# The experts' gathered rows are turned on VectorE in 32x32 blocks instead of on TensorE, and the last product is written as three matmuls

## The chip, the core and the metric

The kernel runs on one core of a Trainium2 chip. Its engines are TensorE (PE, matmuls; PEld is its weight load), VectorE (DVE), ScalarE (ACT), GpSimd (POOL) and SyncE (SP, which only issues transfers). The metric is device time in microseconds. The kernel before takes 1703.79 us, the median of three runs (1703.66 to 1705.21).

## The reference

Input is x, 8 batches of 1024 rows of 256 values. Everything is fp32.

```
xn = layernorm(x)
out = x + attention(xn) + ffn(xn)

attention: layer norm with weights, 16 heads of 16, rope, softmax over 1024 keys, output projection
ffn:  affinity = softmax(xn @ gate_w)                    # 8 experts
      gating, index = top_k(affinity per expert, 256)    # each expert takes 256 rows of each batch
      x_sel = xn[index]
      h = silu(x_sel @ Wg[e]) * (x_sel @ Wu[e])          # 256 -> 512
      contrib = (h @ Wd[e]) * gating                     # 512 -> 256
      out[index] += contrib
```

## The kernel before, in words

The program is one instruction stream for each engine, written out by hand; engines wait for each other through counting semaphores. It has two parts. The first (to about 1126 us) is attention with the router. The second is the experts, and only this one changes.

The experts' work is cut into 32 units: 8 experts of 4 units, each unit 512 gathered rows (ST = 4 tiles of 128). `bp` is the unit's number in its expert. POOL gathers a unit's rows from the normalised rows in DRAM by four indirect transfers (L694) into one of two buffers `xs`, two units ahead, and scatters a unit's results with four accumulating indirect transfers (L705).

fp32 products are made of three products of fp32r parts: each operand is a high part (a cast) and a low part (the difference), and high x high, low x high and high x low are added. So each weight and each activation is split: ACT casts to the high part, DVE subtracts to get the low part.

For one unit the engines do this:
- PE, `turn(unit + 1)` (L1098): the next unit's rows must lie with their 256 values along the partitions. Eight 128x128 transposes write them into the two banks `xt_ps` (L1105).
- ACT and DVE, `turned` (L773, L1452): high and low part of the turned rows, `x_hi` and `x_lo`, two 128x512 operations each.
- PE, `gate_up(unit)` (L1108): for each of four chunks f of the 512 hidden values, 6 matmuls into a gate bank and 6 into an up bank, 512 columns each (L1118). The banks alternate with f, so chunk f waits for h of chunk f - 2 (`need(pe, h_done, FC * unit + f - 1)`).
- ACT takes silu of the gate (L786); DVE multiplies by up, h(f) (L1467); ACT casts, high(f) (L780); DVE subtracts, low(f) (L1459).
- PE, `down(unit)` (L1122): for each row tile t and chunk f, one matmul of 512 columns of the high part of h against both parts of the down weights side by side (L1129), and one of 256 columns of the low part (L1131). A row tile's bank has so two halves of 256 that must be added.
- ACT scales one half by the gating value (L795); DVE scales the other and adds, `y` (L1481). Then POOL scatters.
- In the first three units of each expert but the last, ACT casts one of the next expert's three weights at the end of the unit (`high_weights`, L771), and DVE subtracts (`low_weights`, L1450).

DVE's queue is in order, so where an operation stands in `expert_unit` (L1461) decides what it delays. PE's order in a unit is gate_up, turn of the next unit, down. In units 0 and 1 DVE also prepares the last batch's output projection (`invert`, `quarter_split`), which PE runs in four jobs of 12 matmuls (L946), two behind unit 0 and two behind unit 1, in the banks `xt_ps`.

Of the kernel before, what the change touches and what calls it, by code (L numbers as in the profile page):

```python
# [8 lines left out]
ALU = mybir.AluOpType  # L9
# [6 lines left out]
P = 128  # L16
# [6 lines left out]
NPART = 2  # L23
LANE = 64
LANES = P // LANE
NPAIR = HPG // LANES
# [90 lines left out]
def program(nc, ctx, g):  # L117
# [93 lines left out]
    def tall(half):  # L211
# [13 lines left out]
             [wide(k_stack[0][:, 1, :]), wide(k_stack[0][:, 0, :]), tall(q_stack[1][:, 1, :])]]  # L225
    wd_both = [parts_of[:, :, :].rearrange("p k (f n) -> p k f n", f=FC) for parts_of in (zn_lo, q_stack[1])]
    xs = [qk[:, 2 * i:2 * i + 2, :].rearrange("p i (t n) -> p (i t) n", n=D) for i in range(2)]
    x_hi, x_lo = (k_stack[1][:, i, :].rearrange("p (c n) -> p c n", c=DC) for i in range(2))
    silu, h = [probs[1][:, i, :] for i in range(2)], [probs[1][:, 2 + i, :] for i in range(2)]
    h_hi = parts[1][:, :, :, :].rearrange("p k a n -> p (k a) n")  # L230
# [6 lines left out]
    def rows_ps(t):  # L237

        return (d_ps[0], d_ps[1], g_ps[(FC - 1) % 2], u_ps[(FC - 1) % 2])[t]

# [5 lines left out]
    scattered = [sem(f"scattered{i}") for i in range(UNITS)]  # L246
    xt_full, x_high, x_split = sem("xt_full"), sem("x_high"), sem("x_split")
    gate_full, up_full, silu_done, h_done, h_high, h_split = (
        sem(n) for n in ("gate_full", "up_full", "silu_done", "h_done", "h_high", "h_split"))
    down_full, y_scaled, y_begun = sem("down_full"), sem("y_scaled"), sem("y_begun")  # L250

# [126 lines left out]
    LOW_CYCLE = (28, 29, 30)  # L378
    END_BANKS = {("wo", q): (q // 2, q % 2) for q in range(QUARTERS)}
    ROUTER_CYCLE = (9, 19)  # L380
# [260 lines left out]
    def _(pool):  # L641
# [122 lines left out]
    def _(act):  # L764
# [8 lines left out]
        def turned(unit):  # L773
            for c in range(DC):
                act.wait_ge(xt_full, DC * unit + c + 1)
                act.copy(x_hi[:, c, :], xt_ps[c]).then_inc(x_high, 1)

# [4 lines left out]
        def expert_unit(unit):  # L782
            e, bp = unit // UNITS, unit % UNITS
            for f in range(FC):
                act.wait_ge(gate_full, FC * unit + f + 1)
                act.activation(silu[f % 2], g_ps[f % 2], ACT.Silu).then_inc(silu_done, 1)  # L786
                if f > 0:
                    high(unit, f - 1)
            high(unit, FC - 1)
            if unit + 1 < E * UNITS:  # L790
                turned(unit + 1)
            need(act, scattered[(bp - 2) % UNITS], ST * DMA * (e + (bp >= 2)))
            for t in range(ST):
                act.wait_ge(down_full, ST * unit + t + 1)
                act.activation(y[unit % 2][t], rows_ps(t)[:, D:2 * D], ACT.Copy,  # L795
                               scale=gates_flat[:, e * COLS + bp * ST + t:e * COLS + bp * ST + t + 1]).then_inc(y_begun, 1)
            if bp < WEIGHTS and e + 1 < E:
                high_weights(e + 1, bp)
# [83 lines left out]
    def _(pe):  # L882
# [214 lines left out]

        def turn(unit):  # L1098
            pe.wait_ge(gathered[unit % 2], ST * DMA * (unit // 2 + 1))
            for c in range(DC):  # L1100
                need(pe, x_split, DC * unit + c - 1)
                if unit in (2, 3):
                    pe.wait_ge(side_free, end_jobs.done(("wo", 2 * (unit - 2) + c)))
                for t in range(ST):
                    last = pe.transpose(xt_ps[c][:, t * P:(t + 1) * P], xs[unit % 2][:, t, c * P:(c + 1) * P], ident_sb[:, :])  # L1105
                last.then_inc(xt_full, 1)

        def gate_up(unit):  # L1108
            k = unit // UNITS % 2
            pe.wait_ge(x_split, DC * unit + DC)  # L1110
            for f in range(FC):
                need(pe, h_done, FC * unit + f - 1)
                if f == (FC - 1) % 2:
                    need(pe, y_scaled, ST * unit)
                for w, bank, full in ((GATE, g_ps, gate_full), (UP, u_ps, up_full)):
                    for i, (wt, xt) in enumerate(((we_hi, x_hi), (we_lo, x_hi), (we_hi, x_lo))):
                        for c in range(DC):
                            last = pe.matmul(bank[f % 2], wt[k][w][:, c, f * P:(f + 1) * P], xt[:, c, :],  # L1118
                                             start=i == 0 and c == 0, stop=i == 2 and c == DC - 1)
                    last.then_inc(full, 1)  # L1120

        def down(unit):  # L1122
# [12 lines left out]

            for t in range(2):
                need(pe, y_scaled, ST * (unit - 1) + t + 1)
                part(t, range(FC - 2))
# [8 lines left out]
        turn(0)  # L1147
        weigh(NB - 1, STEPS - 2)
        weigh(NB - 1, STEPS - 1)
        for unit in range(E * UNITS):  # L1150
            if unit % UNITS == 0:
                pe.wait_ge(w_split, WEIGHTS * (unit // UNITS + 1))
            gate_up(unit)
            if unit + 1 < E * UNITS:
                turn(unit + 1)
            if unit == 0:
                pe.wait_ge(o_copied, NB * 2 * NG)
                pe.wait_ge(side_free, end_jobs.base)
            down(unit)
            for job in END_JOBS:  # L1160
                if END_BANKS[job][0] == unit:
                    pe.wait_ge(x_split, DC * (unit + 1) + END_BANKS[job][1] + 1)
                    run_job(end_jobs, job, None, NB - 1, xt_ps[END_BANKS[job][1]])


    @block.vector
    def _(dve):
# [284 lines left out]
        def turned(unit):  # L1452
            for c in range(DC):
                dve.wait_ge(x_high, DC * unit + c + 1)
                dve.tensor_tensor(x_lo[:, c, :], xt_ps[c], x_hi[:, c, :], ALU.subtract).then_inc(x_split, 1)

# [4 lines left out]
        def expert_unit(unit):  # L1461
            e, bp, par = unit // UNITS, unit % UNITS, unit % 2
            for f in range(FC):
                dve.wait_ge(silu_done, FC * unit + f + 1)
                dve.wait_ge(up_full, FC * unit + f + 1)
                need(dve, h_split, FC * unit + f - 1)
                dve.tensor_tensor(h[f % 2], u_ps[f % 2], silu[f % 2], ALU.mult).then_inc(h_done, 1)  # L1467
                if f > 0:
                    low(unit, f - 1)
            low(unit, FC - 1)  # L1470
            if unit + 1 < E * UNITS:
# [6 lines left out]

            for t in range(ST):
                dve.wait_ge(y_begun, ST * unit + t + 1)  # L1480
                dve.scalar_tensor_tensor(y[par][t], rows_ps(t)[:, 0:D],  # L1481
                                         gates_flat[:, e * COLS + bp * ST + t:e * COLS + bp * ST + t + 1], y[par][t],
                                         ALU.mult, ALU.add).then_inc(y_scaled, 1)
            for job in END_JOBS:
                if END_BANKS[job][0] == unit:
                    take(end_jobs, job, None, NB - 1, xt_ps[END_BANKS[job][1]])
# [257 lines left out]
        turned(0)  # L1744
        copy_o(NB - 1, 2 * NG - 1)
        for unit in range(E * UNITS):
            expert_unit(unit)
# [41 lines left out]
```

## Time and profile before

| | |
|---|---|
| median of the runs | 1703.79 us |
| profiled execution, whole | 1702.51 us |
| its span | 1700.7 us |
| PE, DVE, ACT, POOL busy | 98%, 63%, 73%, 31% |
| granted PE clock, mean | 0.991 of full |
| experts' part | about 1126 us to the end |

Busy shares are averages over both parts. An engine's idle time costs something only where another engine waits for what it does next; a busy PE in the profile is a stream of overlapping matmuls, so its pace is read from the starts, not from one matmul's duration.

### The profile page before, as it was taken

Reading aid. Unit: us, or ns where it says so; the run is one execution under the profiler, and the core shown is the slowest. Engines: PE = TensorE matmul, PEld = TensorE weight load, DVE = VectorE, ACT = ScalarE, POOL = GpSimd, SP = SyncE. Lnnn points to the kernel's source line nnn. Section 1 sums busy time; section 2 is a strip of 40 time slices with the busy share of each in tenths; the row PEclk is TensorE's granted clock in tenths of the full one; section 3 lists DMA queues with packets and bytes.
Section 4 is the critical chain, followed back from the end, with each engine's and each line's share of the span. In section 5 each row is a group of like instructions: output and inputs, shape, how many; then the busy total and the mean of one; then the engine's idle time right before and its main releaser. Section 6 shows DMA issues by size and latency. Waiting matters only on the chain.

```text
span 1700.7 us, 28137 instructions
## 1 busy us (share of the span) xinstructions
PE 1659.8 (98%) x10616; PEld 921.9 (54%) x10616; DVE 1076.0 (63%) x2350; ACT 1247.7 (73%) x1544; POOL 522.7 (31%) x480
## 2 busy tenths in 40 slices
PE   6799999999999999999999999999999999999997
PEld 5234344334433433433434433358888888888886
DVE  8874586487477467568558648866455555455543
ACT  5698988998898899899898899964444444444443
POOL 3121111101211111112112100036666565666653
PEclk9799999999999999999999999999999999999998
DMA  5644745764574475465474466345444444434332
GB/s 183 163 102 119 151 98 115 176 129 107 149 169 110 121 159 143 112 145 138 119 161 103 116 139 142 61 146 105 102 94 63 96 78 84 97 65 94 65 57 33
DMA packets 113984, 196.02 MB, mean 115 GB/s; under 512 B 20896, under 2 KB 59680, under 8 KB 113696
## 3 DMA queue, kind: packets, MB, share of 16 engines
q1 hardware_dynamic: 83696, 143.01, 36.6%
q0 software_dynamic: 29040, 49.83, 14.9%
q8 instruction: 101, 1.65, 0.4%
q10 hardware_dynamic: 1088, 1.05, 0.2%
q14 instruction: 59, 0.48, 0.1%
HBM read 117.27 MB, written 76.55 MB: 114 GB/s over the span
## 4 chain that ended last, share of the span: by engine, by line
PE 93%; DVE 4%; DMA 1%; POOL 1%; issue 1%; ACT 0%; POOLq 0%; DVEq 0%; ACTq 0%
PE o_ps L1036 28%; PE score L1118 21%; PE score L1022 20%; PE side L905 5%; PE score L1129 3%; PE side L915 3%; PE side L946 3%; PE o_ps L1129 2%; PE score L1131 2%; PE side L1129 2%; PE score L1105 2%; PE side L889 1%; PE o_ps L1131 1%; PE side L1131 1%; DMA probs<-in_wk_t 0%
## 5 line engine op out<-in xcount | busy, mean ns | idle before, releaser
L807 ACT ACTIVATE probs<-score 128x1024 f32<-128x1024 f32 x1024 | 967.8, 1063 | 103.4 <-PE score L1022 101.1
L1036 PE MATMUL o_ps<-probs,v_ones 128*32 128x512 f32 x4096 | 523.8, 604 | 0.8 <-DVE o_sb L1516 0.6
L1022 PE MATMUL score<-q_stack,k_stack 50*128 50x512 f32 x2048 | 395.6, 458 | 5.1 <-issue 4.5
L1022 PEld LDWEIGHTS score<-q_stack,k_stack 50*128 50x128 f32 x2048 | 164.0, 185 | 353.1 <-ACT probs L807 310.3
L705 POOL DMA_INDIRECT out<-probs,rot x128 | 212.3, 1658 | 189.1 <-DVE probs L1481 159.8
L786 ACT ACTIVATE probs<-score 128x512 f32<-128x512 f32 x128 | 76.7, 599 | 186.8 <-PE score L1118 186.8
L1467 DVE TENSOR_TENSOR probs<-score,probs 128x512 f32<-128x512 f32 x128 | 88.6, 692 | 181.0 <-PE score L1118 176.6
L1036 PEld LDWEIGHTS o_ps<-probs,v_ones 128*32 128x32 f32 x4096 | 92.2, 108 | 200.0 <-issue 139.2
L683 POOL TENSOR_TENSOR square<-qk 128x512 bf16<-128x512 f32 x56 | 77.2, 1407 | 387.6 <-DVE qk L1320 387.6
L694 POOL DMA_INDIRECT qk<-xn_rows,rot x128 | 135.5, 1059 | 38.3 <-issue 29.3
L1118 PE MATMUL score<-k_stack,zn_hi 128*128 128x512 f32 x512 | 140.1, 390 | 0.0
L1118 PE MATMUL score<-k_stack,q_stack 128*128 128x512 f32 x512 | 140.0, 390 | 0.0
L1516 DVE COPY o_sb<-o_ps 128x512 f32<-128x512 f32 x64 | 44.3, 692 | 125.8 <-PE o_ps L1036 125.8
L659 POOL TENSOR_SCALAR ve<-mv 128x4 f32<-128x4 f32 x28 | 6.4, 228 | 336.0 <-DVE mv L1174 336.0
L1118 PEld LDWEIGHTS score<-k_stack,zn_hi 128*128 128x128 f32 x512 | 95.0, 188 | 20.4 <-issue 0.8
L1118 PEld LDWEIGHTS score<-k_stack,q_stack 128*128 128x128 f32 x512 | 95.0, 188 | 19.7
L780 ACT CAST parts<-probs 128x512 fp32r<-128x512 f32 x128 | 78.6, 614 | 33.6 <-DVE probs L1467 33.6
L1118 PE MATMUL score<-k_stack 128*128 128x512 f32 x256 | 79.0, 390 | 0.0
L1118 PE MATMUL score<-k_stack,parts 128*128 128x512 f32 x256 | 79.0, 390 | 0.0
L795 ACT ACTIVATE probs<-score,rot 128x256 f32<-128x256 f32 x64 | 30.4, 476 | 55.9 <-PE score L1131 55.9
L675 POOL COPY v_ones<-v_sb 128x512 f32<-128x512 f32 x32 | 19.7, 614 | 162.6 <-DVE v_sb L1389 85.7
L1459 DVE TENSOR_TENSOR w_hi<-probs,parts 128x512 fp32r<-128x512 f32 x96 | 65.4, 682 | 0.0
(274 smaller groups left out, 2382.7 us busy)
## 6 DMA issues: line engine op xcount, KB each, us to landing
q_parts<-parts SPq DMA_DIRECT2D x16, 1024.0 KB, 4.3
k_parts<-parts SPq DMA_DIRECT2D x16, 1024.0 KB, 7.4
q_stack<-q_parts SPq DMA_DIRECT2D x62, 256.0 KB, 7.1
k_stack<-k_parts SPq DMA_DIRECT2D x62, 256.0 KB, 8.8
q_stack<-q_parts SPq DMA_DIRECT2D x66, 128.0 KB, 7.4
k_stack<-k_parts SPq DMA_DIRECT2D x66, 128.0 KB, 8.1
o_sums<-o_sb SPq DMA_DIRECT2D x256, 32.0 KB
num<-o_sums SPq DMA_DIRECT2D x32, 256.0 KB
```

The source lines that it names most:

```text
L683: last = pool.tensor_tensor(square[i][:, :], qk[:, i, :], qk[:, i, :], ALU.mult)
L694: pool.indirect_dma_start(xs[par][:, t, :], None, xn_dram[:, :], bass.IndirectOffsetOnAxis(ap=rows_now[bp][:, t:t + 1], axis=0))\
L705: pool.indirect_dma_start(out[:, :], bass.IndirectOffsetOnAxis(ap=rows_now[bp][:, t:t + 1], axis=0), y[par][t], None, compute_op=ALU.add)\
L780: act.copy(h_hi[:, f, :], h[f % 2]).then_inc(h_high, 1)
L786: act.activation(silu[f % 2], g_ps[f % 2], ACT.Silu).then_inc(silu_done, 1)
L807: act.activation(probs[probs_of(b, s)][:, 2 * i:2 * i + 2, :], score[ring_of(b, p)][:, :, :], ACT.Exp, scale=SCALE).then_inc(exp_done, 1)
L905: last = pe.matmul(bank[:, :], wt[:, c, a * P:(a + 1) * P], zt[:, c, th * HALF:(th + 1) * HALF], start=i == 0 and c == 0, stop=i == 2 and ...
L1022: last = pe.matmul(score[ring_of(b, p)][:, w, :], k_stack[par][rows, i, kt * P:(kt + 1) * P], q_stack[par][rows, i, qh * HALF:(qh + 1) * H ...
L1036: last = pe.matmul(o_ps[j * KEYS_W:(j + 1) * KEYS_W, :], v_ones[par][:, kt, j, :], probs[probs_of(b, s)][:, j, :], start=kt == 0, stop=kt ...
L1118: last = pe.matmul(bank[f % 2], wt[k][w][:, c, f * P:(f + 1) * P], xt[:, c, :], start=i == 0 and c == 0, stop=i == 2 and c == DC - 1)
L1129: pe.matmul(rows_ps(t).rearrange("p (k n) -> p k n", k=2), h_hi[:, f, at], wd_both[k][:, :, f, :], start=f == 0, stop=False)
L1467: dve.tensor_tensor(h[f % 2], u_ps[f % 2], silu[f % 2], ALU.mult).then_inc(h_done, 1)
```

## The change

The rows of the next unit are turned by DVE. A DVE transpose turns 32x32 blocks in place; to get a whole transpose the program picks the blocks' places: `turn_rows(unit, a)` takes the 32 partitions of row block a and writes its blocks to the four quarters q of the partitions, in four instructions of 32 partitions by 256 elements. Four calls (a = 0 to 3) turn a unit, into the SBUF table of the rotary cosines, no longer needed. `x_hi` and `x_lo` are then made by one 128x1024 operation each. Unit 0 is still turned by PE. Call a = 0 stands at the end of `expert_unit` two units ahead, a = 1 at its beginning one unit ahead, a = 2 and 3 behind h(0) and h(1). The last product has three matmuls of 256 columns for each t and f, all into one half of 256, so ACT alone scales to `y`. Row tiles 2 and 3 go to the banks `xt_ps`, now free; the projection jobs follow gate_up of units 1 and 2.

```diff
@@ rows_ps
-        return (d_ps[0], d_ps[1], g_ps[(FC - 1) % 2], u_ps[(FC - 1) % 2])[t]
+        return (d_ps[0], d_ps[1], xt_ps[0], xt_ps[1])[t]
@@ gather (POOL)
-            need(pool, xt_full, DC * (unit - 1))
+            if unit == 2:
+                pool.wait_ge(xt_full, DC)
+            elif unit > 2:
+                pool.wait_ge(rows_turned, unit - 2)
@@ turned (ACT), unit > 0
+                act.wait_ge(rows_turned, unit)
+                act.wait_ge(up_full, FC * unit)
+                act.copy(x_hi[:, :, :], x_turned).then_inc(x_high, 1)
@@ expert_unit (ACT)
-                act.activation(y[unit % 2][t], rows_ps(t)[:, D:2 * D], ACT.Copy,
-                               scale=...).then_inc(y_begun, 1)
+                act.activation(y[unit % 2][t], rows_ps(t)[:, 0:D], ACT.Copy,
+                               scale=...).then_inc(y_scaled, 1)
@@ gate_up (PE)
-                if f == (FC - 1) % 2:
-                    need(pe, y_scaled, ST * unit)
@@ down (PE)
-                    pe.matmul(rows_ps(t).rearrange("p (k n) -> p k n", k=2), h_hi[:, f, at], wd_both[k][:, :, f, :],
-                              start=f == 0, stop=False)
-                    last = pe.matmul(rows_ps(t)[:, 0:D], h_lo[f][:, at], we_hi[k][DOWN][:, f, :],
-                                     start=False, stop=f == FC - 1)
+                    for i, (ht, wt) in enumerate(((h_hi[:, f, at], we_hi), (h_lo[f][:, at], we_hi), (h_hi[:, f, at], we_lo))):
+                        last = pe.matmul(rows_ps(t)[:, 0:D], ht, wt[k][DOWN][:, f, :],
+                                         start=i == 0 and f == 0, stop=i == 2 and f == FC - 1)
-            for t in range(2):
+            for t in range(ST):
                 need(pe, y_scaled, ST * (unit - 1) + t + 1)
...
                 part(t, range(FC - 2))
-            for t in range(2):
-                part(t, (FC - 2,))
-            for t in range(2):
-                part(t, (FC - 1,)).then_inc(down_full, 1)
-            for t in range(2, ST):
-                part(t, range(FC)).then_inc(down_full, 1)
+            if unit + 1 < E * UNITS:
+                for t in range(ST):
+                    part(t, (FC - 2,))
+                for t in range(ST):
+                    part(t, (FC - 1,)).then_inc(down_full, 1)
+            else:
+                for t in range(ST):
+                    part(t, (FC - 2, FC - 1)).then_inc(down_full, 1)
@@ the loop over units (PE)
             gate_up(unit)
-            if unit + 1 < E * UNITS:
-                turn(unit + 1)
@@ DVE
+        def turn_rows(unit, a):
+            if unit >= E * UNITS:
+                return
+            if a == 0:
+                dve.wait_ge(gathered[unit % 2], ST * DMA * (unit // 2 + 1))
+                dve.wait_ge(x_split, splits_of(unit - 1))
+            rows = slice(a * BLOCK, (a + 1) * BLOCK)
+            from_rows = xs[unit % 2][rows, :, :].rearrange("p t (c q n) -> p q c t n", c=DC, n=BLOCK)
+            to_cols = x_turned.rearrange("p c (t a k) -> p a c t k", t=ST, k=BLOCK)
+            for q in range(BLOCKS):
+                last = dve.transpose(to_cols[q * BLOCK:(q + 1) * BLOCK, a, :, :, :], from_rows[:, q, :, :, :])
+            if a == BLOCKS - 1:
+                last.then_inc(rows_turned, 1)
@@ expert_unit (DVE)
+            turn_rows(unit + 1, 1)
             for f in range(FC):
...
                 dve.tensor_tensor(h[f % 2], u_ps[f % 2], silu[f % 2], ALU.mult).then_inc(h_done, 1)
+                if f + 2 < BLOCKS:
+                    turn_rows(unit + 1, f + 2)
                 if f > 0:
                     low(unit, f - 1)
+            for job in END_JOBS: ...
             low(unit, FC - 1)
             if unit + 1 < E * UNITS:
                 turned(unit + 1)
...
-            for t in range(ST):
-                dve.wait_ge(y_begun, ST * unit + t + 1)
-                dve.scalar_tensor_tensor(y[par][t], rows_ps(t)[:, 0:D], ..., y[par][t],
-                                         ALU.mult, ALU.add).then_inc(y_scaled, 1)
             if bp < WEIGHTS and e + 1 < E:
                 low_weights(e + 1, bp)
+            turn_rows(unit + 2, 0)
```

## Rows read from the trace of the kernel before

**Rows 1.** The page's first lines: span, and PE's busy time, share and instructions.
```profile
span 1700.7 us, 28137 instructions
PE 1659.8 (98%) x10616; PEld 921.9 (54%) x10616; DVE 1076.0 (63%) x2350; ACT 1247.7 (73%) x1544; POOL 522.7 (31%) x480
```
**Rows 2.** Windows: busy time of each engine, granted clock, DMA share, GB/s.
```profile
1200.00:1400.00 200.00, 200.00 (x1016) 169.88 (x1015) 105.95 (x170) 91.97 (x171) 128.15 (x103) 1.00 0.42 77
```
**Rows 3.** The chain of waits in the experts' part: start, duration, what.
```profile
1126.45 11.12 PE score L1118 x48
...
1186.83 10.93 PE score L1118 x48
...
1204.19 10.91 PE score L1118 x48
...
1440.70 0.88 PE score L1105 x8
...
1672.73 10.92 PE score L1118 x48
```
**Rows 4.** PE's waits from 1120 to 1700 us: total, times, longest.
```profile
PE score L946 <- DVE at_lo L1536: 1.8, 2, 0.9
PE score L1105 <- DMA qk<-xn_rows,rot: 1.6, 1, 1.6
```
**Rows 5.** Timeline, PE, output projection, 256 columns: start, duration, instruction, count.
```profile
1060.88 0.39 PE L946 MATMUL side<-w_hi,at_lo 128*128 128x256 f32 x2
...
1061.79 0.39 PE L946 MATMUL side<-w_lo,at_hi 128*128 128x256 f32 x2
...
1144.57 0.40 PE L946 MATMUL score<-w_lo,at_hi 128*128 128x256 f32 x2
...
1145.28 0.40 PE L946 MATMUL score<-w_lo,at_hi 128*128 128x256 f32 x2
```
**Rows 6.** Groups of DVE by shape (busy, mean ns, idle before), and one timeline row.
```profile
L1467 DVE TENSOR_TENSOR probs<-score,probs 128x512 f32<-128x512 f32 x128 | 88.6, 692 | 181.0 <-PE score L1118 176.6 <-ACT probs L786 2.8 <-issue 0.7
...
L1389 DVE TENSOR_TENSOR v_sb<-side,bv_sb 128x256 f32<-128x256 f32 x56 | 21.1, 418 | 68.9 <-PE side L915 68.9
...
L1262 DVE STREAM_TRANSPOSE znT<-side 128x128 f32<-128x128 f32 x15 | 4.5, 299 | 0.7 <-PE side L896 0.7
...
566.68 0.74 DVE L1389 TENSOR_TENSOR v_sb<-side,bv_sb 128x256 f32<-128x256 f32 x2
```
**Rows 7.** Timeline, DVE, two copies on all partitions.
```profile
1110.65 0.28 DVE L1427 COPY rot<-side 128x128 f32<-128x128 f32 x1
1110.85 0.28 DVE L1428 COPY rot<-side 128x128 f32<-128x128 f32 x1
```
**Rows 8.** Timeline, DVE, four operations alternating between lower and upper 64 partitions.
```profile
1106.24 0.28 DVE L1413 CAST rot<-top_row 64x256 f32<-64x256 uint32 x1
1106.56 0.29 DVE L1414 CAST rot<-top_row 64x256 f32<-64x256 uint32 x1
1106.88 0.29 DVE L1415 COPY rot<-top_gate 64x256 f32<-64x256 f32 x1
1107.18 0.29 DVE L1416 COPY rot<-top_gate 64x256 f32<-64x256 f32 x1
```
**Rows 9.** Timeline, all engines, where one unit ends and the next begins.
```profile
1306.56 1.61 POOL L705 DMA_INDIRECT out<-probs,rot  x1 [3.94 <-DVE probs L1481]
...
1308.14 0.63 PE L1118 MATMUL score<-k_stack,zn_hi 128*128 128x512 f32 x2
1308.34 0.48 ACT L795 ACTIVATE probs<-score,rot 128x256 f32<-128x256 f32 x1 [0.91 <-PE score L1131]
...
1308.72 1.04 ACT L771 CAST q_stack<-xn 128x1024 fp32r<-128x1024 f32 x1
...
1309.79 1.23 DVE L1450 TENSOR_TENSOR k_stack<-xn,q_stack 128x1024 fp32r<-128x1024 f32 x1 [0.45 <-ACT q_stack L771]
...
1311.15 0.69 DVE L1467 TENSOR_TENSOR probs<-score,probs 128x512 f32<-128x512 f32 x1
```
**Rows 10.** Timeline, POOL, the last gather in that unit.
```profile
1319.01 0.96 POOL L694 DMA_INDIRECT qk<-xn_rows,rot  x1 [0.30 <-issue]
```
**Rows 11.** Timeline, the start: last issue of gather 0, PE's turn, last of gather 1.
```profile
1118.71 0.95 POOL L694 DMA_INDIRECT qk<-xn_rows,rot  x1 [0.30 <-issue]
...
1123.54 1.06 PE L1105 MATMUL score<-ident_sb,qk 128*128 128x128 f32 x8 [1.55 <-DMA qk<-xn_rows,rot]
...
1125.10 0.95 POOL L694 DMA_INDIRECT qk<-xn_rows,rot  x1 [0.30 <-issue]
```
**Rows 12.** Timeline, DVE in unit 0: inversion, end of the quarter splits, PE behind them.
```profile
1140.85 0.54 DVE L1521 RECIPROCAL den_rec<-den 128x64 f32<-128x64 f32 x1
...
1145.77 0.69 DVE L1536 TENSOR_TENSOR at_lo<-num,at_hi 128x512 fp32r<-128x512 f32 x1
...
1146.61 0.48 PE L946 MATMUL score<-w_hi,at_hi 128*128 128x256 f32 x2 [0.93 <-DVE at_lo L1536]
```

More of the change, by code:

```diff
@@ L24 @@
 LANE = 64
+BLOCK = 32
+BLOCKS = P // BLOCK
 LANES = P // LANE
@@ L237, in rows_ps, with splits_of @@
     def rows_ps(t):
-        return (d_ps[0], d_ps[1], g_ps[(FC - 1) % 2], u_ps[(FC - 1) % 2])[t]
+        return (d_ps[0], d_ps[1], xt_ps[0], xt_ps[1])[t]
+    def splits_of(unit):
+        return DC + unit
     row_cast, row_added, top_merged, top_spread = (
@@ L247, in program @@
     xt_full, x_high, x_split = sem("xt_full"), sem("x_high"), sem("x_split")
+    rows_turned = sem("rows_turned")
     gate_full, up_full, silu_done, h_done, h_high, h_split = (
         sem(n) for n in ("gate_full", "up_full", "silu_done", "h_done", "h_high", "h_split"))
-    down_full, y_scaled, y_begun = sem("down_full"), sem("y_scaled"), sem("y_begun")
+    down_full, y_scaled = sem("down_full"), sem("y_scaled")
     const_in, table_in = sem("const_in"), sem("table_in")
@@ L378, in program @@
     LOW_CYCLE = (28, 29, 30)
-    END_BANKS = {("wo", q): (q // 2, q % 2) for q in range(QUARTERS)}
+    END_BANKS = {("wo", q): (q // 2 + 1, q % 2 + 2) for q in range(QUARTERS)}
     ROUTER_CYCLE = (9, 19)
@@ L773, in turned @@
         def turned(unit):
-            for c in range(DC):
-                act.wait_ge(xt_full, DC * unit + c + 1)
-                act.copy(x_hi[:, c, :], xt_ps[c]).then_inc(x_high, 1)
+            if unit == 0:
+                for c in range(DC):
+                    act.wait_ge(xt_full, c + 1)
+                    act.copy(x_hi[:, c, :], xt_ps[c]).then_inc(x_high, 1)
+            else:
+                act.wait_ge(rows_turned, unit)
+                act.wait_ge(up_full, FC * unit)
+                act.copy(x_hi[:, :, :], x_turned).then_inc(x_high, 1)
         def high(unit, f):
@@ L794, in expert_unit @@
                 act.wait_ge(down_full, ST * unit + t + 1)
-                act.activation(y[unit % 2][t], rows_ps(t)[:, D:2 * D], ACT.Copy,
-                               scale=gates_flat[:, e * COLS + bp * ST + t:e * COLS + bp * ST + t + 1]).then_inc(y_begun, 1)
+                act.activation(y[unit % 2][t], rows_ps(t)[:, 0:D], ACT.Copy,
+                               scale=gates_flat[:, e * COLS + bp * ST + t:e * COLS + bp * ST + t + 1]).then_inc(y_scaled, 1)
             if bp < WEIGHTS and e + 1 < E:
@@ L1096, in _, with turn_first @@
         attend(NB - 1, None, NB - 2)
-        def turn(unit):
-            pe.wait_ge(gathered[unit % 2], ST * DMA * (unit // 2 + 1))
+        def turn_first():
+            pe.wait_ge(gathered[0], ST * DMA)
             for c in range(DC):
-                need(pe, x_split, DC * unit + c - 1)
-                if unit in (2, 3):
-                    pe.wait_ge(side_free, end_jobs.done(("wo", 2 * (unit - 2) + c)))
                 for t in range(ST):
-                    last = pe.transpose(xt_ps[c][:, t * P:(t + 1) * P], xs[unit % 2][:, t, c * P:(c + 1) * P], ident_sb[:, :])
+                    last = pe.transpose(xt_ps[c][:, t * P:(t + 1) * P], xs[0][:, t, c * P:(c + 1) * P], ident_sb[:, :])
                 last.then_inc(xt_full, 1)
@@ L1109, in gate_up @@
             k = unit // UNITS % 2
-            pe.wait_ge(x_split, DC * unit + DC)
+            pe.wait_ge(x_split, splits_of(unit))
             for f in range(FC):
                 need(pe, h_done, FC * unit + f - 1)
-                if f == (FC - 1) % 2:
-                    need(pe, y_scaled, ST * unit)
                 for w, bank, full in ((GATE, g_ps, gate_full), (UP, u_ps, up_full)):
@@ L1153, in _ @@
             gate_up(unit)
-            if unit + 1 < E * UNITS:
-                turn(unit + 1)
+            for job in END_JOBS:
+                if END_BANKS[job][0] == unit:
+                    pe.wait_ge(y_scaled, ST * (unit - 1) + END_BANKS[job][1] + 1)
+                    run_job(end_jobs, job, None, NB - 1, rows_ps(END_BANKS[job][1]))
             if unit == 0:
@@ L1159, in _ @@
             down(unit)
[L1160 to L1163, printed above, removed]
     @block.vector
@@ L1452, in turned @@
         def turned(unit):
-            for c in range(DC):
-                dve.wait_ge(x_high, DC * unit + c + 1)
-                dve.tensor_tensor(x_lo[:, c, :], xt_ps[c], x_hi[:, c, :], ALU.subtract).then_inc(x_split, 1)
+            if unit == 0:
+                for c in range(DC):
+                    dve.wait_ge(x_high, c + 1)
+                    dve.tensor_tensor(x_lo[:, c, :], xt_ps[c], x_hi[:, c, :], ALU.subtract).then_inc(x_split, 1)
+            else:
+                dve.wait_ge(x_high, splits_of(unit))
+                dve.tensor_tensor(x_lo[:, :, :], x_turned, x_hi[:, :, :], ALU.subtract).then_inc(x_split, 1)
+        def turn_rows(unit, a):
[11 more added lines that the diff above has]
+                last.then_inc(rows_turned, 1)
         def low(unit, f):
@@ L1461, in expert_unit @@
         def expert_unit(unit):
-            e, bp, par = unit // UNITS, unit % UNITS, unit % 2
+            e, bp = unit // UNITS, unit % UNITS
+            turn_rows(unit + 1, 1)
             for f in range(FC):
@@ L1467, in expert_unit @@
                 dve.tensor_tensor(h[f % 2], u_ps[f % 2], silu[f % 2], ALU.mult).then_inc(h_done, 1)
+                if f + 2 < BLOCKS:
+                    turn_rows(unit + 1, f + 2)
                 if f > 0:
                     low(unit, f - 1)
+            for job in END_JOBS:
+                if END_BANKS[job][0] == unit:
+                    take(end_jobs, job, None, NB - 1, rows_ps(END_BANKS[job][1]))
             low(unit, FC - 1)
@@ L1745, in _ @@
         copy_o(NB - 1, 2 * NG - 1)
+        turn_rows(1, 0)
         for unit in range(E * UNITS):
```

13 lines of the change are left out of this document (6 added, 7 removed).

## The prediction

> **What bounds the kernel now.** I read the page first: the span is 1700.7 us and TensorE (PE) is busy in 98% of it [rows 1]. The change touches only the experts' part, which starts near 1126 us, so I read that part by itself. Between 1200 and 1400 us PE is busy in all of the 200 us at full clock, VectorE (DVE) in 106, ScalarE (ACT) in 92, GpSimd (POOL) in 128 [rows 2]. The chain of waits shows a strict period: a unit's 48 gate and up matmuls begin at 1204.19 and, 27 units on, at 1672.73, so one unit is 468.54/27 = 17.353 us [rows 3]. In PE's own waits of the whole part there are three: 0.93 us twice on a split of the output projection and 1.6 us on the first gather [rows 4]. So PE's instruction stream is the bound, and DVE's place in it is a deadline, not a share.
>
> **What leaves PE.** Eight turns of gathered rows in each of 31 units (unit 0 keeps its own) take 0.875 us on the chain [rows 3]; their 272 ns each is pipelined. Gate and up stay: 10.92 us, 0.2275 us a matmul. The rest of the unit is the last product, 17.353 - 10.92 - 0.875 = 5.56 us for 16 pairs of a 512-column and a 256-column matmul. It becomes 48 matmuls of 256 columns, each behind its own weight load. The output projection has that very form: four pairs in 0.91 us in one place, three pairs in 0.71 us in another, 0.114 to 0.118 us each [rows 5]. I take 0.117: 5.62 us, bounds 5.47 and 5.66. Unit after, if nothing stalls: 16.54 us, 0.81 less.
>
> **What comes to DVE.** Off: four scaled additions of 0.48 us a unit. On: 16 transposes, each 32 partitions by 256 elements, in four groups of four. Their price decides the case, and no row shows this shape. Nearest is the transpose of 128x128 from PSUM, 299 ns [rows 6]; 128 elements more at the rate between DVE's 256- and 512-element rows ((692 - 418)/256 = 1.07 ns) make 0.43. Other 256-element operations with SBUF sources take 0.41. I take a duration of 0.42 us.
>
> What the queue pays is start to start. Plain back-to-back operations overlap: two of 256 elements end 0.74 us after the first starts, so they start 0.32 apart (0.74 less one's 0.42) [rows 6], and two copies of 128x128 with 0.28 start 0.20 apart [rows 7]. But the list code's operations, which alternate between the lower and the upper 64 partitions, start 0.32, 0.32 and 0.30 us apart with durations of 0.28 to 0.29 [rows 8]: there the next starts only when the last has ended. The transposes write four different quarters of the partitions in turn, and each group reads another one. So I take 0.44 us from start to start, a group of four 1.76 us; bounds 0.30 (the 64x256 copies' rate) and 0.48 (the scaled additions' full duration).
>
> The Trainium skill states this as a rule that speaks against the change (VectorE: DVE Perf Modes, section Two Vector instructions with no wait between them): an instruction whose input or output begins in another group of 32 partitions than the last one's is held until all earlier ones have finished. The trace agrees with 0.30 to 0.32 us against 0.20 [rows 7, 8]. Without the rule the sum below would be the rival at 0.34.
>
> **Where it lands in DVE's order.** Groups 2 and 3 of a unit stand behind h(0) and h(1), where DVE was idle. Groups 0 and 1 for the unit after next and the next stand together in front of h(0), and behind the low weight part of the next expert, which waits for ACT. That is the place. In before, counted from a unit's first matmul (1308.14): ACT scales the last rows at +0.20, casts the weights at +0.58; DVE subtracts at +1.65 to +2.88; h(0) follows at +3.01, when up(0) is full [rows 9]. PE needs h(0) only for its third chunk, at 24 x 0.2275 = +5.46: a slack of about 1.7 us.
> After: the last four row tiles fill 0.35 apart and ACT takes one in 0.37 to 0.38 (0.38 from its last scaling to the cast [rows 9]), so the cast moves to about +0.65 and the subtraction ends at +2.95. Two groups, 3.52 us and the hold ahead of them: +6.50. h(0) 0.69: +7.19, PE goes on some 0.1 later (0.15 behind the quarter split's end [rows 12]), +7.27. Stall 1.81 us.
> Then two more groups: h(1) ends +9.67, group 3 +11.46, low(0) +12.14, h(2) starts +12.07, low(1) ends +13.37. PE, shifted, is through its gates at +12.73 and wants low(1) at +13.08: another 0.37 us. Such a unit is 16.54 + 2.18 = 18.72 us.
> It happens behind every unit with a low weight part: the first three of each of seven experts, 21 in all.
> The other units have no such queue: x_split for the next unit is ready near +14.9, 1.7 us before PE wants it, and their two groups start when the gather lands. POOL's first scatter moves from -1.58 [rows 9] to about -0.1, and its 13.4 us of scatters and gathers, from the first scatter to the last gather's end [rows 9, 10], end at +13.3; with about 4 us to land (the first gather: last issue done at 1119.66, PE released at 1123.54 [rows 11]) the groups end at +20.8, h(0) at +21.5, wanted at +22.0. That fits, with 0.6 us lost once near the end.
>
> **Edits at nothing.** The turn's copy and subtraction read SBUF, one 1024-wide each: 1.04 and 1.23 us [rows 9], beside 1.07 and 1.28 for the pairs they replace; PE's last product hides them. Dropped waits on y_scaled and y_begun: PE has no idle row on them [rows 4]. The new wait of PE on y_scaled for tiles 2 and 3 asks for rows finished 10 us before. POOL's wait on turned rows is passed a unit ahead. ACT's new wait for all of up stands behind high(3), which needs it anyway.
>
> **The first units.** Gather 1's last issue ends at 1126.06, so it lands near 1129.8, 3.4 us into unit 0 [rows 11]. Now DVE waits for it ahead of h(0): 3.4 + 3.52 + 0.7 = 7.6 against 5.46, a stall of 2.2 and 0.3 behind it. In units 0 and 1 the 5.0 to 5.5 us of inversion and quarter splits [rows 12] stood where DVE had time; now the two groups come behind them: in unit 1 h(0) is ready 9.3 us in (stall 3.9), in unit 2 7.9 (stall 2.4). With two projections of 1.41 us in each of units 1 and 2 I get 19.0 + 23.3 + 21.8 = 64.1 us for units 0 to 2, against 1186.83 - 1126.45 = 60.4 [rows 3]: +3.7.
> **The tail.** The last unit's first rows are released 2.2 us before PE's end instead of 2.7; scatters then follow each other: +0.5.
>
> **Sum**, against the profiled execution (1702.5 us, span 1700.7): 29 units x -0.81 = -23.5; stalls in 19 of them (two of the 21 are in the first units) x 2.18 = +41.4; first units +3.7; gather +0.6; tail +0.5. Together +22.7: 1725.2. The median of the runs is 1.3 above the profiled one, a difference smaller than what I know of the price of a transpose, so I say **1725**. Each 0.01 us on a transpose is 8 x 0.01 in the first stall and about half that behind it, times 19 to 21: 2 to 3 us.
>
> **Rivals.**
> A, the forecast: two groups of held transposes ahead of h(0) cost more than PE gives back. 0.62.
> B, no hold: 0.34 start to start. Groups 2.72, h(0) ends at +6.39, stall 1.0, nothing behind it: 19 x 1.0 - 23.5 + 1.5 = -3: 1700. For it: most DVE rows overlap [rows 6, 7]. Against: rows 8. 0.13.
> C, faster: the transposes on 32 partitions run like the 64x256 copies (0.29 to 0.32) [rows 8] or cheaper, and the slack covers them. At 0.30 the stall is 8 x 0.30 + 0.06 - 1.69 (the slack less h(0) and the wake) = 0.77 us, 1693; at 0.21 it is gone and PE gives all it can: 1678 to 1680. Against: these copies have one source and no turning, and the transpose row at 128 elements is longer than the copy of its size (299 against 280). 0.16.
> The Trainium skill says of the transpose that it sustains one element per cycle and lane (Vector Engine (DVE) Microarchitecture Reference, section The reshape front-end and per-opcode configuration). By it C would be out; one length in the trace cannot show a rate.
> D, slower still: a gather that lands 2 us later than I take it, behind DVE's now later first scatter. Then the units without a weight part stall too, by 1 us each in 10, and a late h(0) pushes scatters on: 1735 to 1745. For it: POOL idles only 3.9 us in a unit [rows 9]. 0.09.
>
> That a measurement tells this kernel from itself to about 0.2% (3.4 us) sets the three chances. Faster: C and the lower half of B, 0.24. Same: the rest of B, 0.08. Slower: A and D, 0.68. Range 1697 to 1745; A by itself 1712 to 1740.
>
> **What would show it.** In the profile after: transposes of 0.42 us, starting 0.44 apart; PE waiting on h (the gate matmuls' line, released by the multiplication on DVE) 21 times for 1.8 us; units of 18.7 us three times and 16.5 once in each expert; 16.5 throughout the last expert; no PE wait for x_split. If the transposes start 0.34 apart or less, A is wrong and B or C holds. If the waits are there but the time is not, the last product's price is wrong.

## The result and the profile after

The changed kernel takes 1739.64 us, the median of four runs (1739.03 to 1741.48), against 1703.72 for the kernel before: 1.0211 of it, 95% interval 1.0193 to 1.0228. It is slower by 36 us. I had said 1725, range 1697 to 1745. One run of late_old_product below took 3386 us and is left out of its figures; the other runs of each kernel lie within 0.3% of each other.

The page's first lines, which answer to [rows 1]: the span is 37.7 us longer, and PE's busy time 7.3 us shorter.
```profile
span 1738.4 us, 29031 instructions
PE 1652.5 (95%) x10880; PEld 923.2 (53%) x10880; DVE 1236.6 (71%) x2687; ACT 1245.5 (72%) x1513; POOL 521.3 (30%) x480
```
The window that answers to [rows 2]: PE is busy in 184 of 200 us instead of all, VectorE in 158 instead of 106.
```profile
1200.00:1400.00 200.00, 184.07 (x1044) 158.98 (x1043) 157.95 (x283) 84.44 (x147) 120.30 (x99) 1.00 0.42 82
```
PE's waits from 1120 to 1740 us, where [rows 4] had three in all (total, times, longest). There are 22 on h (L1497 is the multiplication), the 21 of the forecast and one in unit 0, and 20 on a low part of h (L1488). There is none on x_split.
```profile
PE score L1128 <- DVE probs L1497: 37.5, 22, 3.5
PE o_ps L1140 <- DVE w_hi L1488: 8.1, 20, 0.4
PE score L1117 <- DMA qk<-xn_rows,rot: 2.2, 1, 2.2
```
The transposes as a group: 436 ns each. Then the timeline of a stalled unit, which answers to [rows 9]. The unit's first matmul starts at 1307.61.
```profile
L1482 DVE STREAM_TRANSPOSE cos_sb<-qk 32x256 f32<-32x256 f32 x496 | 216.1, 436 | 10.8 <-DMA qk<-xn_rows,rot 2.4
```
```profile
1307.61 0.63 PE L1128 MATMUL score<-k_stack,zn_hi 128*128 128x512 f32 x2
...
1308.25 1.06 ACT L781 CAST q_stack<-xin 128x1024 fp32r<-128x1024 f32 x1
...
1309.35 1.22 DVE L1461 TENSOR_TENSOR k_stack<-xin,q_stack 128x1024 fp32r<-128x1024 f32 x1 [3.57 <-ACT q_stack L781]
...
1310.49 3.57 DVE L1482 STREAM_TRANSPOSE cos_sb<-qk 32x256 f32<-32x256 f32 x8
...
1314.07 0.69 DVE L1497 TENSOR_TENSOR probs<-score,probs 128x512 f32<-128x512 f32 x1
...
1314.82 0.73 PE L1128 MATMUL score<-k_stack,zn_hi 128*128 128x512 f32 x2 [1.58 <-DVE probs L1497]
```
The eight transposes stand between the low weight part and h(0), as one block of 3.57 us. VectorE had been idle for 3.57 us before the low weight part, waiting for ScalarE's cast. PE goes on with its third chunk at +7.21 where it could have at +5.46. The same timeline further on shows the second wait:
```profile
1319.14 0.69 DVE L1488 TENSOR_TENSOR w_hi<-probs,parts 128x512 fp32r<-128x512 f32 x1
1319.97 0.69 DVE L1497 TENSOR_TENSOR probs<-score,probs 128x512 f32<-128x512 f32 x1
1320.58 0.68 DVE L1488 TENSOR_TENSOR w_hi<-probs,parts 128x512 fp32r<-128x512 f32 x1
```
These are low(0), h(2) and low(1). h(2) starts 0.83 us behind low(0), not 0.60, since it waits for low(0)'s end (the wait on h_split, because they share a buffer). So low(1) is done at +13.65.

The chain gives the period. An expert, three stalled units and one free, lies between two rows with all 48 matmuls in one piece (1291.22 and 1365.11): 73.89 us. In the last expert, which has no next weights, the units are 16.55 us (1677.19 to 1693.74). A stalled unit is (73.89 - 16.55)/3 = 19.11 us.
```profile
1291.22 10.91 PE score L1128 x48
...
1365.11 10.91 PE score L1128 x48
...
1677.19 10.91 PE score L1128 x48
...
1693.74 10.91 PE score L1128 x48
```

### The profile page after: what moved, and what is told of

Its sections match the earlier page's. It is cut to its first block, busy times and chain, and to the rows that moved or that the text cites. A ratio compares the mean times of both kernels' runs of the same rounds, so it can differ in the third digit from the quotient of the medians.

```text
span 1738.4 us, 29031 instructions
## 1 busy us (share of the span) xinstructions
PE 1652.5 (95%) x10880; PEld 923.2 (53%) x10880; DVE 1236.6 (71%) x2687; ACT 1245.5 (72%) x1513; POOL 521.3 (30%) x480
## 4 chain that ended last, share of the span: by engine, by line
PE 76%; DVE 15%; issue 4%; ACT 3%; POOL 1%; DMA 1%; DVEq 0%; POOLq 0%; ACTq 0%
PE o_ps L1051 28%; PE score L1037 20%; DVE cos_sb L1482 8%; PE score L1128 7%; PE side L920 5%; PE score L1140 4%; PE side L930 3%; PE side L961 2%; PE o_ps L1140 2%; PE side L1140 2%; DVE probs L1497 2%; ACT probs L810 2%; DVE w_hi L1488 2%; PE side L904 1%; ACT q_stack L781 1%
## 5 line engine op out<-in xcount | busy, mean ns | idle before, releaser
L715 POOL DMA_INDIRECT out<-probs,rot x128 | 219.0, 1711 | 227.7 <-ACT probs L810 198.7
L1482 DVE STREAM_TRANSPOSE cos_sb<-qk 32x256 f32<-32x256 f32 x496 | 216.1, 436 | 10.8 <-DMA qk<-xn_rows,rot 2.4
L1128 PE MATMUL score<-k_stack,zn_hi 128*128 128x512 f32 x512 | 146.7, 400 | 23.3 <-DVE probs L1497 23.3
L704 POOL DMA_INDIRECT qk<-xn_rows,rot x128 | 127.3, 995 | 38.3 <-issue 29.3
L1497 DVE TENSOR_TENSOR probs<-score,probs 128x512 f32<-128x512 f32 x128 | 88.6, 692 | 39.0 <-PE score L1128 19.8
L810 ACT ACTIVATE probs<-o_ps,rot 128x256 f32<-128x256 f32 x32 | 15.2, 474 | 77.7 <-PE o_ps L1140 77.7
L1400 DVE TENSOR_TENSOR v_sb<-side,bv_sb 128x256 f32<-128x256 f32 x56 | 21.1, 417 | 68.9 <-PE side L930 68.9
```

The lines of the kernel that those rows point to most:

```text
L715: pool.indirect_dma_start(out[:, :], bass.IndirectOffsetOnAxis(ap=rows_now[bp][:, t:t + 1], axis=0), y[par][t], None, compute_op=ALU.add)\
L1482: last = dve.transpose(to_cols[q * BLOCK:(q + 1) * BLOCK, a, :, :, :], from_rows[:, q, :, :, :])
```

## The experiments

All the runs are compared with runs of the kernel before on the same chip (1703.0 to 1703.1 us; beside the changed kernel it took 1703.7, so a difference from the changed kernel carries that 0.7 us too). Two of them, group_first and one_quarter, were run once each; I read them by their traces. The theories: Q, the place in VectorE's queue; R, VectorE has too much work wherever it stands; P, the last product is what costs; H, transposes on changing quarters are held.

**late_low.** The low weight part moves one unit later, behind x_lo.
```diff
             if unit + 1 < E * UNITS:
                 turned(unit + 1)
+            if 0 < bp and e + 1 < E:
+                low_weights(e + 1, bp - 1)
...
-            if bp < WEIGHTS and e + 1 < E:
-                low_weights(e + 1, bp)
             turn_rows(unit + 2, 0)
```


> The low part of the next expert's weights is made one unit later, in the gap of VectorE behind the next unit's x_lo; nothing else is changed, VectorE has the same work. Theory Q (place in the queue: the subtraction and two groups of transposes stand ahead of h(0)): with the subtraction gone from there, the two groups start when the gather has landed, h(0) is done 4.4 us after that, and TensorE waits only if the gather lands later than 1.1 us into the unit. All units near 16.6 to 16.8 us instead of 19.1, about 1691 us in all. Theory R (VectorE simply has too much work a unit, the place does not matter): no more than 5 us gained, 1735. Theory G (the gather lands late, 2 us or more into the unit): the groups wait for it, units of 17.5 to 18, about 1710 to 1715.

Measured: 1688.94 us, ratio to before 0.992 (0.9904 to 0.9937). PE waits for h three times only, all in the first three units:
```profile
PE score L1128 <- DVE probs L1497: 8.3, 3, 3.8
PE score L1117 <- DMA qk<-xn_rows,rot: 1.3, 1, 1.3
```
Successive units of its chain start 16.55 us apart. VectorE's busy time from 1200 to 1400 us is 173 us, more than in the changed kernel, and PE's is 200. The 51 us between it and the changed kernel were in the place of one operation of 1.2 us that occurs 21 times; R is refuted. This version is also faster than the kernel before, by 14 us.

**group_first.** Group 0 goes ahead of the low weight part, in VectorE's idle time.
```diff
+            turn_rows(unit + 2, 0)
             if bp < WEIGHTS and e + 1 < E:
                 low_weights(e + 1, bp)
-            turn_rows(unit + 2, 0)
```


> Group 0 of the unit after next is put ahead of the low weight part instead of behind it. It shows when the gather lands. Q with a landing about 1 us into the unit: group to +2.8, subtraction to +4.0, group 1 to +5.8, h(0) to +6.5, stall 1.1 instead of 1.75: about 1725. If the gather lands before the unit begins: the subtraction is as early as before, h(0) done at +5.4, no first stall: about 1700. If it lands 2 us in or later: no gain or a loss. R: 1740, unchanged.

Measured: 1709.05 us (one run). VectorE's timeline in it; the next unit begins on PE at 1319.0:
```profile
1317.54 1.79 DVE L1482 STREAM_TRANSPOSE cos_sb<-qk 32x256 f32<-32x256 f32 x4 [0.41 <-DMA qk<-xn_rows,rot]
1320.66 1.23 DVE L1461 TENSOR_TENSOR k_stack<-xn,q_stack 128x1024 fp32r<-128x1024 f32 x1 [1.33 <-ACT q_stack L781]
1321.91 1.78 DVE L1482 STREAM_TRANSPOSE cos_sb<-qk 32x256 f32<-32x256 f32 x4
1323.71 0.69 DVE L1497 TENSOR_TENSOR probs<-score,probs 128x512 f32<-128x512 f32 x1
```
The gather lands at 1317.5, 1.5 us before the next unit begins, and the group is over before the cast. That is the case "before the unit begins" of the expectation: the first wait is gone (three left, in the first units), the second is not (19 of 0.4 us by the list, 0.9 us a unit by the period of 17.44). I had left that second wait out, so my "about 1700" for this case was 9 us short.

**one_quarter.**
```diff
-                last = dve.transpose(to_cols[q * BLOCK:(q + 1) * BLOCK, a, :, :, :], from_rows[:, q, :, :, :])
+                last = dve.transpose(to_cols[a * BLOCK:(a + 1) * BLOCK, q, :, :, :], from_rows[:, q, :, :, :])
```


> All four transposes of a group write the same quarter of the partitions, the one they read, in four different column blocks; so the blocks lie in the wrong place (that part of the computation is changed), the number, size and order of instructions is the same. Theory H (an instruction whose quarter differs from the last one's waits for its end): duration stays 0.436 us, start to start falls from 0.448 to about 0.35 inside a group, h(0) comes 0.6 to 0.75 us sooner, low(1) as well; a stalled unit 17.7 to 18.0 instead of 19.1; about 1712. Rival (a transpose never overlaps the next operation, whatever the quarter): 1739, unchanged.

Measured: 1705.03 us (one run), 35 us under the changed kernel. In VectorE's timeline the block of eight takes 2.83 us instead of 3.57. The second fence is the page's group:
```profile
1314.16 2.83 DVE L1482 STREAM_TRANSPOSE cos_sb<-qk 32x256 f32<-32x256 f32 x8
1317.01 0.69 DVE L1497 TENSOR_TENSOR probs<-score,probs 128x512 f32<-128x512 f32 x1
1317.73 1.41 DVE L1482 STREAM_TRANSPOSE cos_sb<-qk 32x256 f32<-32x256 f32 x4
```
```profile
L1482 DVE STREAM_TRANSPOSE cos_sb<-qk 32x256 f32<-32x256 f32 x496 | 175.7, 404 | 8.4 <-DMA qk<-xn_rows,rot 5.3
```
From start to start that is (2.83 - 0.40)/7 = 0.35 us against (3.57 - 0.44)/7 = 0.45. A transpose now starts before the last one has ended, as H says. One part of my expectation failed: the duration did not stay at 436 ns, its mean is 404 (median 394). H says nothing on that, and why it falls is open. Stalled units are 17.69 us, 1.42 less. The time is 7 us under the 1712 that I expected: of the 35.2 us of span between the two traces 27 are the 19 steady units, and 8.4 lie ahead of unit 3, where TensorE's clock stayed full in this run (more on that below).

**turn_alone.** The turning of the change with the old last product.
```diff
@@ down
-                    for i, (ht, wt) in enumerate(((h_hi[:, f, at], we_hi), (h_lo[f][:, at], we_hi), (h_hi[:, f, at], we_lo))):
...
+                    pe.matmul(rows_ps(t).rearrange("p (k n) -> p k n", k=2), h_hi[:, f, at], wd_both[k][:, :, f, :], ...)
+                    last = pe.matmul(rows_ps(t)[:, 0:D], h_lo[f][:, at], we_hi[k][DOWN][:, f, :], ...)
@@ expert_unit (DVE)
+            for t in range(ST):
+                dve.wait_ge(y_begun, ST * unit + t + 1)
+                dve.scalar_tensor_tensor(y[unit % 2][t], rows_ps(t)[:, 0:D], ...).then_inc(y_scaled, 1)
             if bp < WEIGHTS and e + 1 < E:
                 low_weights(e + 1, bp)
```


> The changed kernel with the old last product: one matmul of 512 and one of 256 columns, ScalarE scales one half, VectorE adds the other (four more operations of 0.48 us, behind x_lo and ahead of the low weight part). Q: the loss is that of the turning alone; TensorE's unit 0.06 us shorter, the additions fit in VectorE's gap, the subtraction waits for ScalarE as before: 1736 to 1741. Theory P (the three-matmul product with 48 weight loads, and ScalarE scaling all at the end, carry a good part of the loss): 1720 or less.

Measured: 1750.08 us, ratio 1.0274 (1.0257 to 1.0291). A miss of 10 us, and the other way from P. The stalled units are 19.03 us, 0.08 shorter (0.06 expected). But the units without a weight part are no longer free. In the last expert the chain reads
```profile
1684.68 5.50 PE score L1129 x24
1702.12 5.48 PE score L1129 x24
```
17.44 us each, broken at the third chunk. I had counted the four additions as filling VectorE's gap. But they wait for ScalarE's scaling at the unit's end, and the two groups stand behind them too. The unit that begins at 1684.5 shows it:
```profile
1684.25 0.48 DVE L1518 SCALAR_TENSOR_TENSOR probs<-o_ps,rot,probs 128x256 f32<-128x256 f32 x1 [1.41 <-ACT probs L811]
...
1685.83 3.57 DVE L1484 STREAM_TRANSPOSE cos_sb<-qk 32x256 f32<-32x256 f32 x8
...
1689.41 0.69 DVE L1499 TENSOR_TENSOR probs<-score,probs 128x512 f32<-128x512 f32 x1
```
h(0) is done 5.6 us into the unit, just too late for the third chunk, and the low part low(1) behind it is late too; that second wait is the larger of the two.

**late_old_product.** late_low and the old last product together (both diffs above).

> The late low part of the weights together with the old last product (a 512-column and a 256-column matmul, VectorE's four additions of 0.48 us behind x_lo). Theory Q: the additions must wait for ScalarE's scaling, the last one ends about 1.3 us into the next unit, and only then come the two groups of transposes; h(0) is done near 1.3 + 3.58 + 0.7 = 5.6 us plus the hold, 0.3 to 0.5 us late, and low(1) behind it again 0.4 late: units of 17.4 us, about 1712 to 1716. So the three-matmul product, which by itself gives nothing, would be worth some 25 us here. Theory P (the products differ only by TensorE's 0.06 us a unit): 1687 to 1690.

Measured: 1718.00 us (median of three), ratio 1.0087 (1.0066 to 1.0109), 2 us above what I expected; from unit 3 on every unit is 17.43 us. The sum of a moved weight part and the old product is 15 us slower than before; with the new product it is 14 us faster. So the three-matmul product, with VectorE's additions gone by it, is worth 29 us here.

**product_alone.** The kernel before with the new product.
```diff
-                               scale=...).then_inc(y_begun, 1) 
+                               scale=...).then_inc(y_scaled, 1) 
-            for t in range(ST):
...
```
The first pair is ScalarE's scaling, the loop taken out is VectorE's additions; the edit of `down` is the three matmuls of the change.

> The kernel before with only the last product changed: three matmuls of 256 columns for each tile and chunk, ScalarE scales alone, VectorE's four additions are gone; TensorE still turns the rows, the banks and the order of the tiles are those of before. Q: TensorE's unit grows by 16 x (3 x 0.1175 - 0.347), 0.06 to 0.09 us; nothing waited for the additions: 2 to 3 us more, 1705 to 1707. Theory P (the 16 added weight loads a unit cost TensorE more than their matmuls hide): 0.3 us a unit or more, 1713 and up. A gain is possible only if VectorE's or ScalarE's order was a bound before: then below 1703.

Measured: 1704.45 us, ratio 1.0009 (0.9999 to 1.0018). By itself it is nothing that can be told from the kernel before. Its units are 17.45 us, 0.10 longer, which is 3 us in all; in the two traces 1.2 of them do not show, since this one reached unit 0 0.7 us earlier and was 0.5 shorter behind the start of unit 31.

**low1_first.**
```diff
-                if f > 0:
+                if f > 0 and f != 2:
                     low(unit, f - 1)
+                if f == 1:
+                    low(unit, 1)
```


> The changed kernel with low(1) ahead of h(2) in VectorE's queue instead of behind it; the rest as it is. The stalled units are 19.11 us in the trace, 16.55 plus two waits of TensorE, 1.75 on h(0) and about 0.8 on low(1). Theory S (the second wait is VectorE's order behind the first one: low(1) stands behind h(2), and h(2) itself waits for the end of low(0)): low(1) comes 0.8 us sooner, the second wait falls to 0 to 0.1, stalled units 18.3 to 18.4; 21 x 0.75 = 16 us less, 1722 to 1726. Rival (the second wait follows from something else, ScalarE's high(1) or h(3)): 1738 to 1740, the wait only changes its name.

Measured: 1727.19 us, ratio 1.0146 (1.0129 to 1.0163), 12.5 us under the changed kernel. The waits of PE on the low part are gone from its list:
```profile
PE score L1128 <- DVE probs L1497: 38.0, 22, 3.5
PE score L1117 <- DMA qk<-xn_rows,rot: 2.0, 1, 2.0
```
The first wait stays as it was. A stalled unit is 18.43 us (three of them 18.47), so the second wait, 0.68 us, was a matter of VectorE's order alone. I had expected 18.3 to 18.4 and 1 to 5 us less in all.

**both_moves.** late_low and low1_first together.

> Both moves: the low part of the weights one unit later, and low(1) ahead of h(2). With the first move TensorE waits for VectorE in the first three units only, so the second has nothing to gain but there: theory Q says 1686 to 1689, 0 to 2 us under the first move alone. Theory R (VectorE's work a unit is the bound, each move frees some of it): another 10 us or more, below 1680.

Measured: 1690.60 us, ratio 0.9928 (0.9912 to 0.9945): the same as late_low within the intervals, though 2 us above what I expected. R, which wanted less than 1680, is refuted again.

**pe_turns_two.** late_low, and PE turns unit 1's rows as well. POOL's waits and the counts of x_split are adapted to it; that part is not shown.
```diff
@@ the loop over units (PE)
             gate_up(unit)
+            if unit == 0:
+                turn_first(1)
@@ turned (ACT and DVE)
-            if unit == 0:
+            if unit < 2:
@@ turn_rows (DVE)
-            if unit >= E * UNITS:
+            if unit >= E * UNITS or unit < 2:
@@ down (PE)
+                if unit == 0 and t >= 2:
+                    pe.wait_ge(x_split, DC + t - 1)
```


> The late low part of the weights, and TensorE turns the rows of unit 1 too (as before, behind the gates of unit 0), so VectorE turns from unit 2 on. In late_low TensorE waits for h(0) 3.8, 2.4 and 2.1 us in units 0, 1 and 2, the first because gather 1 lands at 1130.6, and its granted clock is low for a few us behind the first. Q: the first wait and the low clock go (3.8 and about 1.7 us), TensorE has 0.9 us of turning and up to 0.8 us of wait for x_lo; the waits of units 1 and 2 stay between 1 and 2.5: 2 to 4 us less than late_low, 1684 to 1687. If the waits only move to the next units: no gain, 1688 to 1690.

Measured: 1680.85 us, ratio 0.9875 (0.9857 to 0.9892), 8 us under late_low and more than expected. This is the fastest version, 22 us under the kernel before. PE's waits:
```profile
PE score L1128 <- DVE probs L1501: 2.4, 2, 2.1
PE score L1117 <- DMA qk<-xn_rows,rot: 1.5, 1, 1.5
PE score L1140 <- DVE k_stack L1471: 0.5, 1, 0.5
```
Unit 1's wait fell from 2.4 to 0.3 us too, which I had not expected: h(3) of unit 0 starts on VectorE at 1137.1 and no longer at 1142.5. TensorE's clock, 0.76 over 1138 to 1142 in late_low, is full here from 1118 us on.

## Why the prediction was right, and which terms were off

The likeliest case (A) is what happened, at its place: two groups of held transposes behind the low weight part and ahead of h(0), 21 times. Where the 37.7 us of span are, from the first gate matmul of each unit in both traces:

| stretch | before | after | difference | forecast |
|---|---|---|---|---|
| up to unit 0 | 1126.38 | 1129.32 | +2.9 | 0 |
| units 0 to 2 | 60.3 | 68.75 | +8.5 | +3.7 |
| units 3 to 30 | 485.9 | 512.1 | +26.2 | +19 |
| unit 31 to the end | 28.1 | 28.3 | +0.2 | +0.5 less the last unit's 0.8 |

- PE's unit without a wait: forecast 16.54 us, measured 16.55. The three-matmul product: 0.117 us a matmul in the forecast, 0.1175 (12 in 1.41 us).
- The price of a transpose: forecast 0.42 and 0.44 from start to start, measured 0.436 and 0.45. That the quarter decides is shown by one_quarter. The Trainium skill's rule (VectorE: DVE Perf Modes, section Two Vector instructions with no wait between them) agrees: 0.45 us with changing quarters, 0.35 with one. Rival B, which was this case without the hold, would have been 1700; one_quarter measures 1705. One small thing I had wrong: the first transpose behind the low weight part is not held, it starts 0.08 us before that subtraction ends (1310.49 against 1310.57).
- Rival C (a transpose at the rate of a 64x256 copy, 0.30) is out: 0.45. With the row of 128 elements [rows 6] there are now two lengths: (436 - 299)/(256 - 128) = 1.07 ns an element. That is an estimate, since the shorter one reads PSUM and all 128 partitions. Nothing is gained by the 96 idle partitions: the 128x256 additions of [rows 6] take 418 ns.
- The first wait: forecast 1.81 us, measured 1.75 (+7.21 less +5.46). Behind the wait the first pair of matmuls takes 0.73 us instead of 0.63, so with low1_first, where only this wait is left, it costs the unit 18.43 - 16.55 = 1.88 us.
- The second wait was mis-sized: the forecast has 0.37 us, and taking it away in low1_first saves 19.11 - 18.43 = 0.68. I let h(2) start 0.60 us behind low(0) as it does where nothing holds it; it waits for low(0)'s end, 0.83. That, and the holds of 0.03 us around the groups, put low(1) at +13.65 instead of +13.37. A stalled unit is so 0.39 us longer than the 18.72 of the forecast, and 19 x 0.39 = 7.4 us covers the 7 us by which the steady units were short in the table. The span as a whole was short by 37.7 - 22.7 = 15 us; the other 7.7 are in the point after next.
- The landing of a gather was mis-sized the other way. I took 4 us from the first gather, which lands among other transfers; group_first shows a landing 1.5 us before the next unit. So the 0.6 us lost once, and rival D, fell away.
- The first units and what is before them cost 7.7 us more than forecast. The waits for h(0) in units 1 and 2 were nearly those of the forecast: PE goes on at +9.14 and +7.85 us, forecast +9.36 and +7.9. What I had not in the sum is the granted clock. The second half of the gates, behind each wait, took 8.31 and 7.36 us on the chain, and 5.74 in unit 2 of pe_turns_two at full clock: +2.6 and +1.6. Ahead of unit 0, from PE's turn to the first gate matmul, 4.5 us instead of 2.8: +1.7. These 5.9 us are most of the 7.7; gather 0, on which PE's turn waits, came 1.2 us later, and unit 0 was 0.4 longer than forecast.
- The chances: the rivals that I counted as slower, A and D, add up to 0.71, and I wrote 0.68; the rest is off by as much the other way.

The second halves of the gates in units 1 and 2, on the chain of the changed kernel, and last that of unit 2 in pe_turns_two:
```profile
1157.87 8.31 PE score L1128 x24
...
1182.37 7.36 PE score L1128 x24
```
```profile
1171.92 5.74 PE score L1128 x24
```
The clock, in the windows of the changed kernel, and last the same window of the kernel before (the third figure from the end is the granted clock):
```profile
1126.00:1128.00 2.00, 2.00 (x12) 0.43 (x8) 1.29 (x2) 0.58 (x2) 1.73 (x3) 0.50 0.77 152
...
1158.00:1162.00 4.00, 4.00 (x10) 3.13 (x11) 3.87 (x9) 1.57 (x3) 3.09 (x4) 0.50 0.72 167
```
```profile
1158.00:1162.00 4.00, 4.00 (x27) 3.50 (x26) 2.66 (x5) 2.53 (x5) 2.75 (x3) 1.00 0.86 239
```
In the changed kernel both stretches are at the lower of the two levels, 1.2 GHz; from 1182 to 1190 us, behind the 2.2 us wait of unit 2, the mean is 0.79. The first follows 2.2 us in which PE waited for gather 0 (1.6 us in [rows 4]). I do not put it down to the change: the edit does not touch that transfer, and in late_low, which has the same start, the wait is 1.3 us and the clock full there. The second follows the wait of 3.5 us for h(0) in unit 1; in the kernel before the clock is full in every window from 1118 to 1200 us. Waits of 1.75 us in the steady units left it at 1.00 in the window of 200 us above.

Why units 0 to 2 stall more than the others is as forecast: group 1 of unit 1 waits for its gather (1132.5 in this trace, forecast 1129.8), and the quarter splits stand ahead of the groups. That unit 0's wait was no longer than forecast (1.7 us, forecast 2.2) is luck: the gather came 2.7 us later than forecast and the unit 2.9 us. In late_low, with the same code up to there, unit 0 began at 1125.4 and waited 3.8 us. That it is worth taking the wait for gather 1 away is shown by pe_turns_two.

The 2.9 us ahead of unit 0 are not shown to belong to the change. In the other traces unit 0 begins between 1125.4 and 1128.0 us, also where the code up to there is that of the changed kernel. What stays open is why the clock fell behind some waits and not behind others.

## What to carry to other kernels

An engine that is busy in half of the time is not free where you put the new work: find the next operation in its queue that a busier engine waits for, and count from the last thing that must come before it. Here 7.2 us of work a unit fitted into VectorE once one subtraction of 1.2 us, waiting for another engine's cast, was moved out from between the idle time and the deadline. And of two parts of an edit one can be worth nothing and the other a loss alone, and both a gain together: the product that frees VectorE at the unit's end is worth nothing that can be measured by itself and saves 29 us with the turning, once that stands in the right place.

## What the hardware showed that I had not expected

- A DVE transpose of 32 partitions by 256 fp32 elements takes 436 ns, as much as a full-width operation of that length; three quarters of the lanes idle. It starts 0.45 us behind the last one if the quarter it writes differs, and 0.35 if not (one_quarter); then its own duration is shorter too, 404 ns in the mean.
- PE's granted clock fell to half behind single waits of 2.2 us (before unit 0) and 3.5 us (unit 1), and below full behind 3.8 us in late_low (0.81 over 1134 to 1138), and not behind the 1.75 us waits of the steady units. one_quarter had one of 3.1 us with the clock full, so the length alone does not decide it.
- A gather of 512 rows landed 3.7 us behind the end of its last issue at the start of the experts' part (gather 0 of the kernel before), 5.8 us for gather 1 of the changed kernel (1126.7 to 1132.5), and within about 2 us in the steady part (group_first, 1315.7 to 1317.5).
